# A two-layer decoder on one core: last norms in two parts, routing in pieces between the shared products, slots written out

## The chip, the cores and the metric

The kernel runs on one core of a Trainium2 chip. The metric is the device time of one execution in microseconds; the median of three runs is given beside the time of the one execution that was profiled. Engines are named as in the profile: PE is TensorE, PEld its weight loads, DVE is VectorE, ACT is ScalarE, POOL is GpSimd, SP is SyncE.

## What is computed

Four sequences of 512 tokens with 512 features, 2048 tokens in all, pass six residual parts, each followed by a layer norm without weights. The change touches the last two parts and the norms behind them:

```
x = _layernorm(x + _L1_xattn_ref(ctx_512, x, Wq, Wk, gamma))      # graph stage
x = _layernorm(x + _L1_ffn_ref(x, router_w, router_bias, Wu, Wg, Wd, Su, Sg, Sd))

# graph:  sim >= threshold of the 153 largest of its row; A = sigmoid(sim) * mask
#         A = (A + A transposed) / 2;  result (1 - g) * x + g * A
# experts:
logits = flat @ router_w.T                       # 16 experts
scores = softmax(logits); topk_idx = top_k(logits + router_bias, 2)
combine = the two scores of the chosen experts, divided by their sum
for e in range(16):
    out += combine[:, e:e + 1] * ((silu(flat @ Wu[e]) * (flat @ Wg[e])) @ Wd[e])     # 256 wide
out += (silu(flat @ Su) * (flat @ Sg)) @ Sd                                          # shared, 512 wide
```

## The kernel before

X stays in SBUF as 16 tiles of 128 tokens (four batches of four). Each stage is a block in which every engine has its own straight list of instructions and waits on semaphores; nothing orders the work but these lists and waits. There is a barrier between stages. Before the part that matters here come two self attentions, a cross attention, a quantised feed-forward stage, and a search for the graph's thresholds.

Products that need more than one pass of precision take a matrix as a high part (a copy in the type fp32r) and a low part (the rest); H stands for high, L for low in the names. The high part is written by ScalarE, the low one is a subtraction on VectorE (or POOL), and a product is three matmuls: high by high, low by high, high by low.

**Graph stage** (stage_graph, L1470). A loop over four batches: ScalarE computes SIGM and XS, VectorE masks them (L1584), PE transposes (L1522), VectorE adds (L1591), mixes into X (L1597) and takes statistics (L1600). Behind the loop VectorE computes mean and 1/deviation of all 16 tiles in 25 small steps (L64 to L77, each waits for the one before) and applies them to 16 tiles (L1605).

**route_and_share** (L1637). PE turns X (L1867) into two PSUM places UG; ScalarE and VectorE write XTH and XTL (L1743, L1768). Logits: for each of 16 token tiles twelve matmuls, XT standing in the array and the router's 16 columns moving (L1876). Then VectorE routes: two best experts per token (L1780, L1781), their shares, per-tile counts from PE (L1884, L1885), running sums BEFORE (L1801), first tile of each expert (L1806), slots (L1808 to L1818), the expert of each slot tile (L1823 to L1826). After its last step (semaphore routed at ROUTE) two things start: POOL scatters the token numbers into a table in HBM with 32 indirect DMAs (L1731), which SP then reads back, and VectorE and PE begin the shared expert. That has two halves j of 256 hidden columns; per half the weights are converted in one piece (L1751, L1841), and then for each of four batches m PE does up_gate (48 matmuls, L1895) and down of the batch before (24, L1908); ScalarE does the silu (L1755) and the high part of H (L1758), VectorE the product H (L1848), its low part (L1852) and the addition to X (L1835, gather).

**run_slots** (L1924). Tokens sorted by expert fill 48 tiles of 128 slots, each with one expert. Per tile POOL fetches 128 token rows (XG, L1986) and the expert's weights (RAW, 128 x 3072, L1988) into rings of four places; ScalarE writes WH in three copies (two of the up part L2060, down L2072), VectorE the low part of the first up half (L2089) and of down (L2121), POOL that of the second up half (L1993). PE does twelve up products (L2144), turns the next tokens (L2132) and the hidden rows (L2159), and does six down products (L2178); VectorE copies the result to YS (L2118), SP stores it. The indirect DMAs read their row numbers from PICK, which VectorE fills (L2080, L2081) since the tile's number is a loop variable. The first four and the last five steps are written out, the others run in a loop of four steps. POOL issues the fetch for tile t+3 in step t when down_lo shows tile t-1 done.

**combine_slots** (L2185). POOL gathers two rows per token (32 indirect DMAs, L2207, ring of four), VectorE adds them with their shares (L2216), takes statistics (L2219) and, after the last, norms as in the graph stage (L2224). Behind a barrier store_x writes X in one DMA of 4.2 MB (L2268).

## Time and profile before

| | us |
|---|---|
| median of 3 runs (2809.75 to 2814.63) | 2813.01 |
| the profiled execution | 2814.64 |
| its span, first to last instruction | 2812.7 |
| busy in the span: PE, DVE, ACT, POOL | 2066.3, 1822.6, 1217.9, 801.8 |
| logits, 2167.8 to 2209 | 41.2 |
| routing and first weights, 2209 to 2244.6 | 35.6 |
| shared expert, 2244.6 to 2388.4 | 143.8 |
| slots, 2388.4 to 2735.7 | 347.3 |
| combination, norm and store, 2735.7 to 2812.7 | 77.0 |

Times in the trace count from the start of the span. A window's row gives the busy time of each engine in a stretch, the mean clock that TensorE was granted as a share of 2.4 GHz (0.50 is 1.2 GHz), the share of the time in which packets were under way on the 16 DMA engines (packets may overlap, so it can pass 1) and what they moved. A row of the timeline gives start, duration, engine, line, operation, tiles, the count of merged instructions, and in brackets the idle time of the engine before it with what ended it.

### The profile page before, as it was taken

The page shows a single profiled execution, that of the slowest core. Times are in us where ns is not written, and L with a number is a line of the kernel's source. Part 1 is how long each engine was busy: PE and PEld are TensorE (multiplying, and loading weights), DVE is VectorE, ACT ScalarE, POOL GpSimd, SP SyncE. Part 2 cuts the span into 40 slices and gives each one's busy share as a digit, 9 for nine tenths or more (in the row PEclk, how much of TensorE's full clock was granted, in tenths as well). Part 3 has the DMA queues.
Part 4 walks back from the last instruction along what each step waited for, and adds up shares of the span by engine and source line. Part 5 has one row for each costly group of instructions (what it writes and reads, how often), then busy time and mean ns, then how long its engine had stood idle before and what let it go on. Part 6 is the DMA issues. An engine that isn't in the chain of part 4 may idle for free. (4 is left out here: it accounts for less than half of the span.)

```text
span 2812.7 us, 34294 instructions
## 1 busy us (share of the span) xinstructions
PE 2066.3 (73%) x12308; PEld 1398.0 (50%) x12308; DVE 1822.6 (65%) x2851; ACT 1217.9 (43%) x2168; POOL 801.8 (29%) x712
## 2 busy tenths in 40 slices
PE   5999997386877886899847999994014589677760
PEld 4778775122222223555526777772003477555540
DVE  3456555476767757899963555654885433788876
ACT  2332222285556563677762322321862021556540
POOL 1211322106577511121111212131000130666654
PEclk8999998589889888999967999997555599999995
DMA  4422221655244204000013223221002000899965
GB/s 142 98 56 59 57 58 23 180 173 144 90 127 121 61 12 170 1 1 1 1 38 98 64 50 69 52 62 60 0 0 107 1 1 0 308 307 303 305 223 164
DMA packets 84875, 266.48 MB, mean 95 GB/s; under 512 B 17488, under 2 KB 19024, under 8 KB 73600
## 3 DMA queue, kind: packets, MB, share of 16 engines
q0 software_dynamic: 29856, 153.33, 18.2%
q1 hardware_dynamic: 53856, 111.01, 13.9%
q8 instruction: 89, 1.46, 0.2%
q10 hardware_dynamic: 1024, 0.26, 0.0%
q14 instruction: 50, 0.41, 0.0%
HBM read 171.70 MB, written 41.99 MB: 76 GB/s over the span
## 5 line engine op out<-in xcount | busy, mean ns | idle before, releaser
L875 DVE TENSOR_REDUCE x_negm<-x_M 128x2 f32<-128x1024 f32 x256 | 309.3, 1223 | 115.4 <-PE x_M L935 114.9
L824 ACT ACTIVATE x_PT<-x_T 128x512 f32<-128x512 f32 x512 | 280.2, 598 | 210.8 <-PE x_T L955 206.0
L317 ACT ACTIVATE L_attn_PT<-L_attn_T 128x512 f32<-128x512 f32 x320 | 175.4, 595 | 357.9 <-PE L_attn_T L519 357.7
L387 DVE TENSOR_REDUCE L_attn_negm<-L_attn_M 128x2 f32<-128x1024 f32 (+1 forms) x192 | 191.8, 1041 | 56.5 <-PE L_attn_M L500 56.2
L224 POOL DMA_DIRECT2D L_attn_QKS<-L_attn_HL x64 | 34.9, 546 | 598.0 <-ACT L_attn_HL L302 564.3
L955 PE MATMUL x_T<-x_QS,x_KS 49*128 49x512 f32 x512 | 144.0, 559 | 64.0 <-ACT x_PT L824 43.7
L517 PE MATMUL L_attn_T<-L_attn_QKS 97*128 97x256 f32 (+3 forms) x512 | 164.6, 383 | 10.2 <-DMA L_attn_QKS<-L_attn_mT 7.9
L964 PE MATMUL x_O<-x_PT,x_V 128*32 128x512 f32 x1024 | 160.7, 704 | 7.6 <-issue 7.6
L955 PEld LDWEIGHTS x_T<-x_QS,x_KS 49*128 49x128 f32 x512 | 53.0, 204 | 217.5 <-ACT x_PT L824 135.9
L935 PE MATMUL x_M<-x_KS,x_QS 48*128 48x512 f32 x512 | 120.7, 468 | 42.8 <-DMA x_QS<-x_xl 23.3
L498 PE MATMUL L_attn_M<-L_attn_QKS 96*128 96x384 f32 (+2 forms) x384 | 134.8, 420 | 19.2 <-DVE L_attn_XTL L361 11.5
L1522 PE MATMUL graph_P<-ident,graph_L 128*128 128x128 f32 x64 | 15.7, 428 | 173.0 <-DVE graph_L L1584 167.8
L2060 ACT ACTIVATE slots_WH<-slots_RAW 128x1024 fp32r<-128x1024 f32 x94 | 94.6, 1054 | 100.3 <-DMA slots_RAW<-in_experts,slots_PICK 100.3
L2121 DVE TENSOR_TENSOR slots_WL<-slots_RAW,slots_WH 128x1024 fp32r<-128x1024 f32 x48 | 130.9, 2726 | 0.2 <-ACT slots_WH L2072 0.2
L434 PE MATMUL L_attn_M<-L_attn_XTH,L_attn_WH 128*128 128x512 f32 x256 | 109.1, 426 | 16.3 <-DVE L_attn_XTL L361 16.3
L519 PE MATMUL L_attn_T<-mask_kq,identr 128*128 128x128 f32 x512 | 120.4, 247 | 0.0
L1993 POOL TENSOR_TENSOR slots_WL<-slots_RAW,slots_WH 128x1024 fp32r<-128x1024 f32 x48 | 116.3, 2423 | 10.5 <-ACT slots_WH L2060 5.6
L1534 ACT ACTIVATE graph_seen_a<-graph_SIM,graph_mid 128x512 bf16<-128x512 f32 x128 | 90.5, 708 | 59.1 <-DMA graph_SIM<-graph_sim 39.8
L517 PEld LDWEIGHTS L_attn_T<-L_attn_QKS 97*128 97x128 f32 x512 | 104.8, 205 | 17.0 <-DMA L_attn_QKS<-L_attn_mT 9.1
L405 DVE RECIPROCAL L_attn_AQ<-L_attn_DEN 128x512 f32<-128x512 f32 x32 | 107.2, 3349 | 7.1 <-PE L_attn_O L537 7.1
L434 PE MATMUL L_attn_M<-L_attn_XTH,L_attn_WL 128*128 128x512 f32 x256 | 106.4, 416 | 0.0
L1986 POOL DMA_INDIRECT slots_XG<-moe_x_rows,slots_PICK x48 | 48.6, 1012 | 201.7 <-DVE slots_PICK L2081 200.9
(377 smaller groups left out, 5711.9 us busy)
## 6 DMA issues: line engine op xcount, KB each, us to landing
L_attn_QKS<-L_attn_HL SPq DMA_DIRECT2D x192, 128.0 KB, 4.7
L_attn_QKS<-L_attn_HL POOLq DMA_DIRECT2D x192, 128.0 KB, 4.1
moe_y_rows<-slots_YS SPq DMA_DIRECT2D x48, 256.0 KB, 7.6
x_WRAW<-in_w_gateT POOLq DMA_DIRECT2D x8, 1024.0 KB, 7.5
x_QS<-x_xh SPq DMA_DIRECT2D x128, 64.0 KB, 2.4
x_WRAW<-in_w_upT POOLq DMA_DIRECT2D x8, 1024.0 KB, 5.6
x_WRAW<-in_w_downT POOLq DMA_DIRECT2D x8, 1024.0 KB, 5.9
ffn_w<-x_WTER POOLq DMA_DIRECT2D x12, 512.0 KB, 3.6
```

Source lines behind the costliest of these rows:

```text
L317: ac.activation(PT[:, s, bank], T[:, bank], ACT.Exp, scale=SCALE).then_inc(t_free, 1)
L387: last = ve.tensor_reduce(negm[:, g % 2, h0:h0 + nh, i], src, AX.X, ALU.max, negate=True)
L434: inst = pe.matmul(out, lhs(a, k), rhs(a, k), start=(n == 0), stop=(n == len(passes) - 1))
L498: pe.matmul(m[:, c:c + w], QKS[0:R, r, 0, h, P * i:P * (i + 1)], QKS[0:R, r, 1, h, 0:w], start=True, stop=False)
L517: pe.matmul(T[:, c:c + w], QKS[0:R + 1, r, 1, h, P * j:P * (j + 1)], QKS[0:R + 1, r, 0, h, P * j:S], start=True, stop=False)
L519: last = pe.matmul(T[:, c:c + P], C["identr"][:], C["mask_kq"][:], start=False, stop=True)
L824: ac.activation(PT[:, s // 4, head(s), :], T[(STEPS_S * g + s) % 3][:], ACT.Exp, scale=SCALE).then_inc(t_free, 1)
L875: ve.tensor_reduce(negm[:, g % 2, u // 4:4:2, u % 4], m[:].rearrange("p (r k) -> p r k", r=2), AX.X, ALU.max, negate=True).then_inc(m_free, 1)
L935: last = pe.matmul(m[:, BANK * r:BANK * (r + 1)], QS[rows, g % 4, u // 4, P * (u % 4):P * (u % 4 + 1)], KS[rows, g % KV, :], start=True, s ...
L955: pe.matmul(T[(STEPS_S * g + s) % 3][:], KS[rows, g % KV, P * j:P * (j + 1)], QS[rows, g % 4, head(s) % 2, :], start=True, stop=True).then ...
L964: last = pe.matmul(O[VW * h:VW * (h + 1), :], V[:, (g // KV) % 2, j, g % KV, :], PT[:, j, h, :], start=(j == 0), stop=(j == NT - 1))
L2121: ve.tensor_tensor(WL[i % 2][:, DOWN], RAW[i][:, DOWN], WH[i % 2][:, DOWN].bitcast(F32), ALU.subtract).then_inc(q["down_lo"], 1)
```

## The change

- **Last norms.** In the graph stage and in the combination, the small steps are done in two parts: for tiles 0 to 11 (EARLY = 12) before the last batch's work, for 12 to 15 behind it. A 26th step makes shift = -mean * rstd (emit_shift). ScalarE applies the first 14 tiles (norm_tile), VectorE the last two. The store is part of the combination's block: SP stores each batch when its tiles are done, the last one in two halves. The graph's loop over batches is written out.
- **Turning and logits.** X is turned into four PSUM places (TURN) instead of two. The router's weights stand in the array (16 columns), 512 token columns move: 48 matmuls instead of 192. The result is 16 x 2048; ScalarE copies it out (LT) and PE turns it back by 16 transposes.
- **Routing in pieces.** The shared weights are converted in two pieces (2048 up columns, 1024 down columns), the first pieces directly behind the logits. PE starts the shared products then and does the counting products behind up_gate(0, 1); VectorE's routing is cut into functions that stand between its operations of the shared expert. The counts are copied out of PSUM (take_counts), and PE waits for that before down(0, 0). The second half's weights are converted during the last products of the first.
- **Slots.** All steps are written out; 47 tiles instead of 48; rings of six places; POOL only issues the fetches, with row numbers straight from slot_token and weight_row (no PICK); VectorE does the low part of both up halves; ScalarE copies the result to YS, one step later.

```diff
+            def norm_tile(t):
+                ac.activation(XF[:, t, :], XF[:, t, :], ACT.Identity, scale=rstd[:, t:t + 1],
+                              bias=shift[:, t:t + 1]).then_inc(q["applied"], 1)
...
+            act.wait_ge(q["shifted"], 1)
+            for t in range(EARLY):
+                norm_tile(t)
+            act.wait_ge(q["shifted"], 2)
+            for t in range(EARLY, EARLY + NT // 2):
+                norm_tile(t)
+            act.wait_ge(q["applied"], EARLY + NT // 2)
...
+                if b == NB - 1:
+                    moments(0, 0, EARLY)
...
-    SLOT_TILES = 2 * NTILE + NE
+    SLOT_TILES = 2 * NTILE + NE - 1
...
+        TURN = UG + Y
...
+            for v in range(2):
+                act.wait_ge(q["lt_full"], 2 * v + 2)
+                ac.activation(LT[:, 2 * BANK * v:2 * BANK * (v + 1)], UG[v][0:NE, :], ACT.Copy).then_inc(q["lt_taken"], 1)
+            for part in range(2):
+                weights_hi(0, part)
...
+                assert route.n == TAKEN
+
+            def first_tiles():
+                route(ve.memset(BEFORE[:, 0, :], 0.0))
+                for t in range(NTILE):
+                    route(ve.tensor_tensor(BEFORE[:, t + 1, :], BEFORE[:, t, :], COUNT[:, t, :], ALU.add))
...
+            weights_lo(0, 0)
...
+            best_two(0, 8)
+            hidden(0, 0, 0)
+            best_two(8, NTILE)
+            hidden(0, 0, 1)
+            choices()
+            hidden_lo(0, 0, 0)
+            hidden_lo(0, 0, 1)
+            weights_lo(0, 1)
+            hidden(0, 1, 0)
+            shares()
+            hidden(0, 1, 1)
+            take_counts()
+            hidden_lo(0, 1, 0)
+            hidden_lo(0, 1, 1)
...
+            first_tiles()
+            for i in range(NT):
+                gather(0, 0, i)
+            hidden(0, 2, 0)
+            slot_places()
+            hidden(0, 2, 1)
+            hidden_lo(0, 2, 0)
+            hidden_lo(0, 2, 1)
+            for i in range(NT):
+                gather(0, 1, i)
+            tile_experts()
...
+                if m == NB - 1:
+                    if j == 0:
+                        weights_lo(1, 0)
+                    for i in range(NT):
+                        gather(j, m, i)
+                    if j == 0:
+                        weights_lo(1, 1)
...
+                if n >= 4:
+                    t_.wait_ge(q["xt_lo"], n - 3)
...
-            for t in range(NTILE):
+            for b in range(NB):
+                t_.wait_ge(q["xt_lo"], max(2 * b + 2, 5 + b // 2))
+                if b >= 2:
+                    t_.wait_ge(q["xt_lo"], 2 * NB)
                 n = 0
-                for xp, wp in ((XTH, RWL), (XTL, RWH), (XTH, RWH)):
+                for wp, xp in ((RWL, XTH), (RWH, XTL), (RWH, XTH)):
                     for k in range(KC):
-                        last = pe.matmul(Y[0][:, NE * t:NE * (t + 1)], xp[:, k, P * t:P * (t + 1)], wp[:, k, :],
-                                         start=(n == 0), stop=(n == 3 * KC - 1))
+                        last = pe.matmul(UG[b // 2][0:NE, BANK * (b % 2):BANK * (b % 2 + 1)], wp[:, k, :],
+                                         xp[:, k, S * b:S * (b + 1)], start=(n == 0), stop=(n == 3 * KC - 1))
                         n += 1
+                last.then_inc(q["lt_full"], 1)
+            for v in range(2):
+                t_.wait_ge(q["lt_taken"], v + 1)
+                for t in range(2 * NT * v, 2 * NT * (v + 1)):
+                    last = pe.transpose(Y[0][:, NE * t:NE * (t + 1)], LT[:, P * t:P * (t + 1)], C["ident"][0:NE, 0:NE])
             last.then_inc(q["logits"], 1)
...
-            t_.wait_ge(q["routed"], ROUTE)
-            with t_.Fori(0, 2) as j:
-                t_.wait_ge(q["w_lo"], j + 1)
+            for j in range(2):
                 for m in range(NB):
                     up_gate(j, m)
+                    if j == 0 and m == 1:
+                        t_.wait_ge(q["made"], 8)
+                        t_.wait_ge(q["routed"], SORTED)
+                        mask = MASK[:].rearrange("p t e -> p (t e)")
+                        pe.matmul(Y[1][:, 0:NTILE * NE], earlier[:], mask, start=True, stop=True)
+                        pe.matmul(Y[1][:, BANK:BANK + NTILE * NE], ones[:], mask, start=True,
+                                  stop=True).then_inc(q["counted"], 1)
+                        t_.wait_ge(q["routed"], TAKEN)
                     if m > 0:
                         down(j, m - 1)
                 down(j, NB - 1)
...
-    RING = 4
-    TURNS = SLOT_TILES // RING
+    RING, LAST = 6, SLOT_TILES - 1
...
-                        if not isinstance(t, int):
-                            pool.sem_inc(q["between"], 1)
-                        pool.wait_ge(q["down_lo"], t)
-                        if not isinstance(t, int):
-                            pool.sem_inc(q["between"], 1)
-                        pool.wait_ge(q["up_lo_pool"], t)
-                    if not isinstance(t, int):
-                        pool.sem_inc(q["between"], 1)
-                    fetch(t + RING - 1, i + RING - 1)
...
+            for t in range(SLOT_TILES):
+                n = t % RING
+                if t >= RING:
+                    pool.wait_ge(down_lo, t - RING + 1)
+                    pool.wait_ge(up_lo, 2 * (t - RING + 1))
+                pool.indirect_dma_start(out=XG[n], out_offset=None, in_=T["x_rows"],
+                                        in_offset=bass.IndirectOffsetOnAxis(T["slot_token"][:, t:t + 1], 0)
+                                        ).then_inc(x_in[n], 16)
+                pool.indirect_dma_start(out=RAW[n], out_offset=None, in_=weights,
+                                        in_offset=bass.IndirectOffsetOnAxis(T["weight_row"][:, t:t + 1], 0)
+                                        ).then_inc(w_in[n], 16)
...
+            def take_y(t):
+                act.wait_ge(y_full, t + 1)
+                if t >= 4:
+                    act.wait_ge(y_out[t % 4], 16 * (t // 4))
+                ac.activation(YS[t % 4], Y[t % 2][:], ACT.Copy).then_inc(y_taken, 1)
+
+            up_weights(0)
+            turned(0)
+            for t in range(SLOT_TILES + 2):
+                if t < LAST:
+                    up_weights(t + 1)
+                if 1 <= t <= SLOT_TILES:
+                    act.wait_ge(ht_full, t)
+                    ac.activation(HH[:], HT[:, 0:F], ACT.Copy).then_inc(h_hi, 1)
+                if t >= 2:
+                    take_y(t - 2)
+                if t < LAST:
+                    turned(t + 1)
+                if t <= LAST:
+                    act.wait_ge(u_full, t + 1)
+                    ac.activation(SU[t % 2], U[t % 2][:, 0:F], ACT.Silu).then_inc(silu_done, 1)
+                    if t >= 2:
...
+            for t in range(SLOT_TILES + 1):
+                if t < LAST:
+                    up_rest(t + 1, 0)
+                if t >= 1:
+                    dve.wait_ge(h_hi, t)
+                    ve.tensor_tensor(HL[:], HT[:, 0:F], HH[:].bitcast(F32), ALU.subtract).then_inc(h_lo, 1)
+                if t < LAST:
+                    up_rest(t + 1, 1)
+                    turned_rest(t + 1)
+                if t <= LAST:
+                    dve.wait_ge(silu_done, t + 1)
+                    ve.tensor_tensor(H[t % 2], SU[t % 2], U[t % 2][:, F:], ALU.mult).then_inc(h_made, 1)
+                    dve.wait_ge(down_hi, t + 1)
+                    ve.tensor_tensor(WL[t % 2][:, DOWN], RAW[t % RING][:, DOWN], WH[t % 2][:, DOWN].bitcast(F32),
+                                     ALU.subtract).then_inc(down_lo, 1)
...
             for t in range(NTILE):
+                if t == EARLY:
+                    moments(0, 0, EARLY)
...
+            moments(1, EARLY, NTILE)
+            for t in range(EARLY + NT // 2, NTILE):
+                ve.tensor_scalar(XF[:, t, :], XF[:, t, :], mean[:, t:t + 1], rstd[:, t:t + 1],
+                                 ALU.subtract, ALU.mult).then_inc(applied_v, 1)
...
+        @block.sync
+        def _(sp):
+            for b in range(NB - 1):
+                sp.wait_ge(applied_a, NT * (b + 1))
+                sp.dma_start(out[:, b, :, :], X[:, b, :, :]).then_inc(x_out, 16)
+            sp.wait_ge(applied_a, EARLY + NT // 2)
+            sp.dma_start(out[:, NB - 1, 0:NT // 2, :], X[:, NB - 1, 0:NT // 2, :]).then_inc(x_out, 16)
+            sp.wait_ge(applied_v, NT // 2)
+            sp.dma_start(out[:, NB - 1, NT // 2:, :], X[:, NB - 1, NT // 2:, :]).then_inc(x_out, 16)
+            sp.wait_ge(x_out, 16 * (NB + 1))
```

**TensorE, from the turning of X to the first shared product.** Before (share_UG and share_Y are PSUM places, the last two numbers the shape written):

```order
L1867 MATMUL share_UG<-ident,X 128x128 x64
L1876 MATMUL share_Y<-share_RWL,share_XTH 128x16 x4
L1876 MATMUL share_Y<-share_RWH,share_XTL 128x16 x4
L1876 MATMUL share_Y<-share_RWH,share_XTH 128x16 x4
...
L1884 MATMUL share_Y<-share_routing,share_earlier 128x256
L1885 MATMUL share_Y<-share_routing,share_ones 128x256
```

After:

```order
L1967 MATMUL share_Y<-ident,X 128x128 x16
L1978 MATMUL share_UG<-share_XTH,share_RWL 16x512 x4
L1978 MATMUL share_UG<-share_XTL,share_RWH 16x512 x4
L1978 MATMUL share_UG<-share_XTH,share_RWH 16x512 x4
...
L1985 MATMUL share_Y<-ident,share_LT 128x16 x16
L1999 MATMUL share_UG<-share_XTH,share_WH 128x512 x4
```

The group of three rows of logits stands 16 times before and 4 times now, and the counting products no longer stand between the logits and the first shared product.

**VectorE, from the sorted choices on.** Before:

```order
L1791 TENSOR_TENSOR share_routing<-share_routing 128x256
L1793 TENSOR_TENSOR share_total<-moe_share 128x16
L1794 RECIPROCAL share_total<-share_total 128x16
L1796 TENSOR_TENSOR moe_share<-moe_share,share_total 128x16 x2
L1799 MEMSET share_BEFORE 128x16
L1801 TENSOR_TENSOR share_BEFORE<-share_BEFORE,share_Y 128x16 x16
L1802 TENSOR_SCALAR share_tiles_i<-share_BEFORE 128x16
L1803 TENSOR_SCALAR share_tiles_i<-share_tiles_i 128x16
L1804 CAST share_tiles_f<-share_tiles_i 128x16
```

After:

```order
L1853 TENSOR_TENSOR share_routing<-share_routing 128x256
L1831 TENSOR_TENSOR share_HL<-share_H,share_HH 128x512 x2
L1819 TENSOR_TENSOR share_WL<-share_RAW,share_WH 128x1024
L1827 TENSOR_TENSOR share_H<-share_SU,share_UG 128x512
L1857 TENSOR_TENSOR share_total<-moe_share 128x16
L1858 RECIPROCAL share_total<-share_total 128x16
L1860 TENSOR_TENSOR moe_share<-moe_share,share_total 128x16 x2
L1827 TENSOR_TENSOR share_H<-share_SU,share_UG 128x512
L1865 COPY share_WITHIN<-share_Y 128x256
L1866 COPY share_COUNT<-share_Y 128x256
L1831 TENSOR_TENSOR share_HL<-share_H,share_HH 128x512 x2
L1870 MEMSET share_BEFORE 128x16
```

The routing's steps keep their order; between them now stand the low parts and products of the shared expert's first two batches, and the two copies out of PSUM.

**VectorE, one step of the slots.** Before (the loop's register instructions left out):

```order
L2080 COPY slots_PICK<-moe_slot_token 128x1
...
L2081 COPY slots_PICK<-moe_weight_row 128x1
...
L2089 TENSOR_TENSOR slots_WL<-slots_RAW,slots_WH 128x1024
L2104 TENSOR_TENSOR slots_HL<-slots_HT,slots_HH 128x256
L2085 TENSOR_TENSOR slots_XTL<-slots_XT,slots_XTH 128x512
L2109 TENSOR_TENSOR slots_H<-slots_SU,slots_U 128x256
L2118 COPY slots_YS<-slots_Y 128x512
L2121 TENSOR_TENSOR slots_WL<-slots_RAW,slots_WH 128x1024
```

After (the two rows of L2148 are the two up halves):

```order
L2148 TENSOR_TENSOR slots_WL<-slots_RAW,slots_WH 128x1024
L2159 TENSOR_TENSOR slots_HL<-slots_HT,slots_HH 128x256
L2148 TENSOR_TENSOR slots_WL<-slots_RAW,slots_WH 128x1024
L2143 TENSOR_TENSOR slots_XTL<-slots_XT,slots_XTH 128x512
L2165 TENSOR_TENSOR slots_H<-slots_SU,slots_U 128x256
L2167 TENSOR_TENSOR slots_WL<-slots_RAW,slots_WH 128x1024
```

The picks and the copy of YS have gone, and a third subtraction of 128x1024 stands between HL and XTL.

## Rows read from the trace of the kernel before

**Rows 1.** Windows by stage: length, busy us (instructions) per engine, clock, DMA share, GB/s.

```profile
core 0: us, PE busy (x) PEld busy (x) DVE busy (x) ACT busy (x) POOL busy (x), PEclk, DMA share, GB/s
2079.00:2149.40 70.40, 15.73 (x64) 12.55 (x64) 55.80 (x97) 18.78 (x32) 0.00 (x0) 0.50 0.00 0
2150.40:2167.80 17.40, 11.33 (x64) 9.52 (x64) 9.78 (x9) 9.51 (x10) 1.31 (x8) 0.79 0.92 328
2167.80:2209.00 41.20, 41.10 (x192) 41.04 (x192) 0.00 (x0) 0.00 (x0) 0.00 (x0) 0.50 0.12 45
2209.00:2244.60 35.60, 2.05 (x5) 1.19 (x5) 29.54 (x129) 5.74 (x4) 3.23 (x1) 0.50 0.00 0
2244.60:2312.30 67.70, 67.69 (x288) 55.52 (x288) 20.50 (x31) 9.39 (x16) 30.96 (x32) 0.97 0.02 2
2312.30:2320.20 7.90, 0.02 (x1) 0.03 (x1) 4.05 (x2) 5.33 (x3) 0.00 (x0) 0.83 0.00 0
...
2400.00:2411.00 11.00, 6.91 (x24) 5.44 (x25) 5.70 (x11) 7.00 (x10) 6.80 (x4) 0.72 1.01 414
...
2440.00:2700.00 260.00, 202.60 (x912) 151.89 (x912) 227.68 (x303) 154.37 (x227) 164.05 (x114) 1.00 0.91 304
...
2735.70:2784.40 48.70, 0.00 (x0) 0.00 (x0) 35.16 (x48) 0.00 (x0) 34.19 (x32) 0.50 0.61 172
...
2801.00:2811.00 10.00, 0.00 (x0) 0.00 (x0) 0.00 (x0) 0.00 (x0) 0.00 (x0) 0.50 1.03 386
```

**Rows 2.** Timeline, end of graph stage: start, us, engine, line, operation, tiles, count, [idle].

```profile
2120.47 2.56 ACT L1550 ACTIVATE graph_XS<-X,graph_g 128x512 f32 x4 [7.86 <-DVE X L1597]
...
2126.02 1.23 DVE L1591 TENSOR_TENSOR graph_SUM<-graph_P,graph_L 128x1024 f32<-128x1024 f32 x1 [2.13 <-PE graph_P L1522]
...
2134.83 0.18 DVE L64 TENSOR_TENSOR graph_mean<-graph_stats 128x16 f32<-128x16 f32 x1
...
2140.08 9.28 DVE L1605 TENSOR_SCALAR X<-X,graph_mean,graph_rstd 128x512 f32<-128x512 f32 x16
```

**Rows 3.** Timeline, VectorE, turning X.

```profile
2154.33 2.35 DVE L1768 TENSOR_TENSOR share_XTL<-share_UG,share_XTH 128x1024 fp32r<-128x1024 f32 x2 [0.69 <-ACT share_XTH L1743]
```

**Rows 4.** Timeline, TensorE, first shared products, low clock, then high.

```profile
2244.59 2.07 PE L1895 MATMUL share_UG<-share_XTH,share_WH 128*128 128x512 f32 x4 [20.21 <-DVE share_WL L1841]
...
2249.56 1.07 PE L1895 MATMUL share_UG<-share_XTH,share_WH 128*128 128x512 f32 x4
```

**Rows 5.** Tile share_WH: duration ns min/median/max, first and last start.

```profile
L1751 ACT ACTIVATE share_WH<-share_RAW x2: 2762/2762/2762, 2212.6 to 2313.8; 128x3072 fp32r x2
...
L1841 DVE TENSOR_TENSOR share_WL<-share_RAW,share_WH x2: 3359/3360/3360, 2241.1 to 2316.7; 128x3072 fp32r<-128x3072 f32 x2
```

**Rows 6.** Tile moe_table: POOL's scatters, same columns.

```profile
L1731 POOL DMA_INDIRECT moe_table<-share_token_id,share_place x32: 957/962/4092, 2241.4 to 2284.0; - x32
```

**Rows 7.** Groups by shape, 2410 to 2720: busy us, mean ns, idle before.

```profile
L2121 DVE TENSOR_TENSOR slots_WL<-slots_RAW,slots_WH 128x1024 fp32r<-128x1024 f32 x46 | 128.4, 2792 | 0.2 <-ACT slots_WH L2072 0.2
...
L2089 DVE TENSOR_TENSOR slots_WL<-slots_RAW,slots_WH 128x1024 fp32r<-128x1024 f32 x46 | 55.7, 1211 | 1.1 <-ACT slots_WH L2060 1.1
...
L2118 DVE COPY slots_YS<-slots_Y 128x512 f32<-128x512 f32 x45 | 31.1, 692 | 37.2 <-PE slots_Y L2178 37.2
...
L2036 ACT ACTIVATE slots_XTH<-slots_XT 128x512 fp32r<-128x512 f32 x45 | 26.8, 595 | 27.1 <-PE slots_XT L2132 26.7
```

**Rows 8.** Waits, 2410 to 2720: us in total, times, longest.

```profile
ACT slots_WH L2060 <- DMA slots_RAW<-in_experts,slots_PICK: 97.2, 44, 3.4
```

**Rows 9.** DMA queues, 2440 to 2700: packets, MB, share of 16 engines.

```profile
q0 software_dynamic: 8464, 69.15, 81.1%
q1 hardware_dynamic: 5468, 9.96, 9.9%
```

**Rows 10.** Timeline, combination: POOL's gather beside VectorE.

```profile
2740.70 1.43 POOL L2207 DMA_INDIRECT combine_YG<-moe_y_rows,moe_slot  x1 [0.30 <-issue]
...
2740.57 1.54 DVE L2216 SCALAR_TENSOR_TENSOR X<-combine_YG,moe_share,X 128x512 f32<-128x512 f32 x2 [8.71 <-DMA combine_YG<-moe_y_rows,moe_slot]
```

564 lines of the change are left out of this document (259 added, 305 removed).

## Prediction

> **What bounds the kernel now.** I read the windows by stage first, since the change touches only the last 734 us of a 2812.7 us span (from the graph stage's normalisation at 2134.8 on), and different things end each stretch there [rows 1]. The reader should see five stretches. (a) The end of the graph stage is VectorE alone. (b) 2167.8 to 2209: TensorE is busy for all of its 41.2 us, but with 192 products of only 16 columns, at a granted 0.50 (1.2 GHz). (c) 2209 to 2244.6: TensorE has 5 matmuls in 35.6 us; VectorE works on the routing and then on the weights' low part. (d) 2244.6 to 2388: shared products back to back, 67.7 us for each of the two weight halves, with a hole of 7.9 us between them. (e) 2440 to 2700, the slots' steady part: 38 tiles in 260 us, 6.84 each; nothing is full (TensorE 5.33 us a tile, VectorE 5.99, ScalarE 4.06, POOL 4.32), and DMA shows a share of 0.91 at 304 GB/s. A tile moves 128 x 3072 x 4 bytes of weights and twice 128 x 512 x 4, 2.10 MB. Then come the combination (POOL 34 of 49 us), the norm and a store that nothing overlaps.
>
> The slots need a closer look. ScalarE waits 97.2 us in 44 times for weights to land [rows 8]: 2.2 us a tile. That does not say yet that bandwidth is the limit. A fetch for tile t+3 goes out only when VectorE has finished tile t-1's down part. One form explains much of VectorE's load: the down subtraction takes 2792 ns, while the same shape on another line takes 1211 [rows 7]. It runs while POOL does its own 128x1024 subtraction; and every time it is late, the next fetch is late. So fetch, conversion, subtraction and fetch form a ring of four places: 27.4 us round, 6.84 a tile.
>
> **The change, part by part**, against the profiled execution (span 2812.7, 2814.6 in all; the median of the runs is 2813.0, 1.6 less).
>
> 1. Graph norm. Before: 25 small steps from 2134.83 to 2140.08 (0.21 each), then 16 tiles in 9.28 us [rows 2]. After: 26 steps for 12 tiles go ahead of the last batch's sums, 5.5 us, of which 2.13 lie in the wait for TensorE that stands there anyway; +3.3. Behind the last statistics 26 steps more, 5.5, then two tiles on each of two engines; ScalarE's take 0.64 each (2.56 for 4 [rows 2]), 1.3. Its first 12 tiles (7.7 us) lie beside VectorE's last 8.8 + 5.5. Sum: 3.3 + 5.5 + 1.3 = 10.1 against 14.5: **-4.4**. Unrolling the four batches itself gains nothing: VectorE shows no gap at a turn.
>
> 2. Turning X. Two PSUM places become four. VectorE then is the bound: eight subtractions at 1.18 (2.35 for two [rows 3]), the first 3.9 us in, done at 13.3 instead of 17.4. TensorE is ahead, done turning after about 10.4. Logits: 48 products of 512 columns instead of 192 of 16. Four such products take 2.07 us from start to end at the low clock and 1.07 at the high one, and follow each other each 0.91 at the latter [rows 4], 0.226 a product: 10.9 us. In the turning of before TensorE was busy 11.3 of 17.4 us, in pieces with waits between, and had a mean of 0.79; now it turns almost without a hole, so I take the high clock. Logits' end comes 10.4 + 10.9 = 21.3 after the start instead of 58.6: **-37.3**. At the low clock the 48 take 21.8, 10.9 more.
>
> 3. From logits to the first shared product. Before 35.6 us [rows 1]: all the routing, then the subtraction of 3.36 [rows 5]. After: the copy of 16x1024 out of PSUM, not in the trace (bounds 0.6, a 128x512 PSUM copy, to 1.1; 1.1 taken, since a 128x1024 PSUM read takes 1.0); conversion of 2048 of 3072 columns, 1.84; its subtraction, 2.24 [rows 5]; 0.15 to start. 5.3 in all: **-30.3**. The 16 small turns hide beside the conversion.
>
> 4. Routing between the shared products. VectorE's routing costs 29.5 - 3.4 = 26 us [rows 1], and it is busy only 20.5 of 67.7 us in a half. Let T be the first product. Walking VectorE's new list with the old durations: the choices (MASK) are ready at T+18; TensorE reaches the counting products at T+24; they take 1.0 to 2.0, and TensorE then waits until VectorE, which first takes hidden(0,1,1), has copied both counts out: T+26.8. **+2.8**. Slots' places are known at T+43, the last step at T+55. POOL then scatters 32 times at 0.96 + 0.3 [rows 6] plus the table's way back, until about T+102, where the shared products run until T+136. Cover left: 33 us; if it is gone, the excess counts in full.
>
> 5. Between the halves. TensorE's 7.9 us hole [rows 1] goes: the first 2048 columns are converted and subtracted during down(0,3), which frees nothing else late. With it goes the restart at the low clock, (2.07 - 1.07) over the first ten or so products, 2.5. **-10.4**.
>
> 6. Slots. One tile fewer, six places instead of four, POOL fetches only, VectorE gets POOL's half and gives the output copy to ScalarE. VectorE a tile: 5.99 - (2.79 - 1.21) - 0.69 (copy [rows 7]) - 0.2 (two picks) + 1.21 = 4.7. ScalarE 4.06 + 0.60 (its PSUM copies of 128x512 [rows 7]) = 4.7. TensorE stays at 5.33. In the loop of TensorE's order, turning the next tokens, ScalarE's copy, VectorE's rest and the next product give 5.2 to 5.3 a tile. DMA: bounds are 5.07 (2.10 MB at the 414 GB/s of 2400 to 2411, when fetches stood in line [rows 1]) and 6.22 (the packets' own time: 81.1% + 9.9% of 6.84 [rows 9]), with 6.84 if nothing improves. With six places fetches stand in line as in the fast stretch, but writes are mixed in as in the slow one: I take 5.6, nearer the former, since in the slow one each fetch waited for VectorE before it was issued, and six places end that. 46 steps of 5.6 against 47 of 6.81: 257.6 against 320.0, **-62.4**. Start and tail stay.
>
> 7. Combination and store. VectorE reaches tile 12 with 12 tiles summed; 26 steps, 5.5, go in ahead of it. POOL's gathers run on meanwhile, so VectorE has the last four tiles in hand and takes 2.3 each; last statistics 4.2 us later than before. Then 5.5 + 1.3, and the last 0.5 MB: 1.4 at 386 GB/s [rows 1] plus 1.5 fixed (the 4.2 MB store landed in 12.4, of which 10.9 are data at that rate). From the old end of statistics 4.2 + 6.8 + 2.9 + 0.8 = 14.7 instead of 28.3: **-13.6**.
>
> Sum: -4.4 - 37.3 - 30.3 + 2.8 - 10.4 - 62.4 - 13.6 = -155.6. 2814.6 - 155.6 - 1.6 = **2657**.
>
> A rule that speaks against part 6. POOL's gather that began at 2740.70 took 1.43 instead of 0.95 and ended at 2742.13, just when VectorE's two operations with two SBUF inputs ended at 2742.11 [rows 10]; others there with the same overlap did too. The Trainium skill (SBUF — State Buffer, SBUF: two separate sides) says that VectorE and GpSimd share a port pair as an exclusive lock, and that GpSimd cannot write the descriptors of its DMAs meanwhile. By that rule, the trace agrees; here it would stretch each fetch and not the sum, since POOL has 5.6 us for two.
>
> **The rivals.**
> A. DMA stays the limit. For it: 0.91 share, ScalarE's waits [rows 8]. Against: 414 GB/s were reached. At 6.22 a tile: 46 x 0.62 = 29 more, 2686; at 6.84 only the one tile is saved: 57 more, 2714.
> B. Engines and DMA are both better than taken: 5.1 to 5.3, 2634 to 2643.
> C. The logits run at the low clock: +11, 2668; it adds to any case.
> D. Slower. In the slots, VectorE now runs three 1.21 us subtractions with two SBUF inputs, 3.6 us a tile. If each of POOL's two fetches were held until all of that has passed, and more fetches did not help: 2 x (1.26 + 3.63) = 9.8 a tile, 46 x 4.2 = 193 more, 2850. It outweighs the other gains from 5.6 + 156/46 = 9.0 a tile on. Against: a held gather lost 0.5, not 3.6, and VectorE's list has three operations a tile with at most one SBUF input.
> E. The pieces don't fit: VectorE is late for the silu products and TensorE stands 10 to 30 us in the first half, or the scatter sticks out. 2667 to 2690. My walk shows one place only.
> F. The change does not do what it says: long straight code is fetched in the slots while the DMA queues are full, and engines stand for it. In 2440 to 2700 of before only one instruction packet was needed; straight code elsewhere ran without such holes, but under less traffic. 1 us a tile would be 46: 2703. The Trainium skill (Runtime: NRT & Kernel Launch, Instruction fetch mechanics) says that straight code is fetched ahead and taken branches are what stalls; no row here shows either under full queues.
>
> **How the numbers follow.** Forecast with 5.3 to 5.9 a tile 0.55 (2643 to 2671); A 0.25; B 0.06; E 0.06; F 0.05; D 0.03; C is inside the others (0.3). A measurement of this kernel tells 0.2% (5.6 us) from no change. All but D and the extremes of F and E end far below that: faster 0.95, same 0.01, slower 0.04. The range reaches from B's floor to A's ceiling: 2634 to 2714.
>
> **What would show each step.** Logits of about 11 us at clock 1.0; the first shared product near 2173; no hole between halves, one of 3 us at the counting products; the last scatter ahead of the last shared product; steady tiles 5.6 apart, VectorE's down subtraction back at 1.21, DMA near 370 GB/s; the last store 0.5 MB. The prediction is wrong if the steady tiles stay above 6.3 apart, if VectorE in the shared stage makes TensorE wait in more than one place, or if POOL's fetches take more than 2 us each.

## The result, and the profile after

The changed kernel takes 2624.3 us, the median of 4 runs (2621.3 to 2635.8), against 2813.8 before (2809.8 to 2814.7): a ratio of 0.936, 95% interval 0.933 to 0.938. The prediction was 2657 with a range of 2634 to 2714: the direction was right, and the time is 9.7 us below the low end. The profiled execution took 2622.4 us with a span of 2620.7, 192.0 less than before's. One later execution of the changed kernel took 3171.7 us at a mean granted clock of 0.617, against 0.867 to 0.872 in all its others, and is left out of every comparison.

The windows by stage of the changed kernel (length, busy us and instructions of each engine, TensorE's clock, DMA share, GB/s), from the first masked product of the graph stage on; the rows of before are in [rows 1]:

```profile
core 0: us, PE busy (x) PEld busy (x) DVE busy (x) ACT busy (x) POOL busy (x), PEclk, DMA share, GB/s
2066.28:2128.20 61.92, 15.74 (x64) 12.55 (x64) 52.16 (x110) 28.08 (x45) 0.00 (x0) 0.50 0.00 0
2128.20:2155.56 27.36, 22.08 (x128) 14.55 (x128) 11.71 (x11) 13.88 (x14) 1.34 (x8) 0.87 0.78 276
2155.56:2293.40 137.84, 134.40 (x580) 110.52 (x580) 73.02 (x197) 23.35 (x36) 33.40 (x32) 0.98 0.01 1
2293.40:2556.70 263.30, 240.96 (x1128) 183.64 (x1128) 230.70 (x282) 215.88 (x329) 131.39 (x94) 0.97 0.92 375
2556.70:2620.70 64.00, 0.00 (x0) 0.00 (x0) 44.80 (x102) 10.09 (x14) 33.71 (x32) 0.50 0.64 197
```

In the third row (the shared expert) the shared products now fill 134.4 of 137.8 us; in the fourth (the slots) TensorE is busy for 241 of 263 us, where before it idled over a fifth of the slots' steady part. Cut at the same marks in both traces, the 192 us go like this:

| stretch (marks) | before, us | after, us | difference | predicted |
|---|---|---|---|---|
| start to the graph's first masked product | 2080.1 | 2066.3 | -13.8 | 0 |
| to the end of the graph's norm | 69.3 | 61.9 | -7.4 | -4.4 |
| to the first shared product | 95.2 | 27.4 | -67.8 | -67.6 |
| to the first slot fetch | 145.4 | 138.1 | -7.3 | -7.6 |
| to the first gather of the combination | 345.7 | 263.1 | -82.6 | -62.4 |
| to the end of the span | 77.0 | 63.9 | -13.1 | -13.6 |

Three rows are off: the first, in code that the change doesn't touch; the second by 3 us; the slots by 20.

How the third row of the table came out is seen in TensorE's timeline (start, us, line, operation, tiles, shapes, count, [idle before]):

```profile
2129.35 3.65 PE L1967 MATMUL share_UG<-ident,X 128*128 128x128 f32 x16 [12.84 <-PEq L48]
...
2139.05 1.09 PE L1978 MATMUL share_UG<-share_XTH,share_RWL 128*16 128x512 f32 x4
...
2149.25 1.09 PE L1978 MATMUL share_UG<-share_XTH,share_RWH 128*16 128x512 f32 x4
...
2151.44 0.67 PE L1985 MATMUL share_Y<-ident,share_LT 16*128 16x16 f32 x8 [0.51 <-ACT share_LT L1796]
2155.56 1.65 PE L1999 MATMUL share_UG<-share_XTH,share_WH 128*128 128x512 f32 x3 [3.46 <-DVE share_WL L1819]
```

Turning takes 9.6 us, the 48 logit products 11.3 at the high clock (four in 0.93), and 5.2 us later the first shared product starts.

The slots' steady part, 2350 to 2500, by groups (busy us, mean ns of one, idle before), to be held against [rows 7]:

```profile
L2148 DVE TENSOR_TENSOR slots_WL<-slots_RAW,slots_WH 128x1024 fp32r<-128x1024 f32 x59 | 71.8, 1217 | 0.0
L2108 ACT ACTIVATE slots_WH<-slots_RAW 128x1024 fp32r<-128x1024 f32 x60 | 60.2, 1059 | 0.0
L2086 POOL DMA_INDIRECT slots_XG<-moe_x_rows,moe_slot_token x29 | 48.9, 1685 | 55.7 <-DVE slots_WL L2167 55.7
...
L2167 DVE TENSOR_TENSOR slots_WL<-slots_RAW,slots_WH 128x1024 fp32r<-128x1024 f32 x30 | 36.8, 1226 | 6.0 <-ACT slots_WH L2137 6.0
```

The down subtraction is back from 2792 ns to 1226. ScalarE's first copy (L2108) has no idle time before it: the wait of 2.2 us a tile for the weights [rows 8] is gone. Now POOL waits, 1.9 us a tile, because the ring is full. The windows' row for the same 150 us names the new bound:

```profile
2350.00:2500.00 150.00, 148.01 (x703) 113.26 (x703) 143.52 (x176) 134.30 (x205) 84.13 (x58) 1.00 1.02 417
```

TensorE is busy for 148.0 of 150 us, VectorE for 143.5. So busy time alone does not say which of the two sets the tile; fewer_products below does. A tile's order on TensorE, one tile of the timeline:

```profile
2452.11 1.17 PE L2186 MATMUL slots_U<-slots_WH,slots_XTH 128*128 128x512 f32 x4
2453.11 1.08 PE L2186 MATMUL slots_U<-slots_WH,slots_XTL 128*128 128x512 f32 x4
2454.03 0.38 PE L2200 MATMUL slots_HT<-ident,slots_H 128*128 128x128 f32 x2
2454.17 1.18 PE L2186 MATMUL slots_U<-slots_WL,slots_XTH 128*128 128x512 f32 x4
2455.18 0.60 PE L2177 MATMUL slots_XT<-ident,slots_XG 128*128 128x128 f32 x4
2455.54 0.71 PE L2218 MATMUL slots_Y<-slots_WH,slots_HH 128*128 128x512 f32 x2
```

There is no idle time in it of 0.1 us or more. The 18 products of 512 columns follow each other at 0.23 us within a group and the six turns at 0.11, which makes 4.8 us (an estimate from these spacings); the rest of the tile goes at the changes from one group to the next. From the first to the last H product on VectorE (2313.4 to 2548.1, 46 steps) a tile takes 5.10 us.

The end, from the timeline: the moments of the first twelve tiles, the last norm and the last store.

```profile
2594.38 0.18 DVE L64 TENSOR_TENSOR combine_mean<-combine_stats 128x12 f32<-128x12 f32 x1
...
2599.97 8.57 ACT L2280 ACTIVATE X<-X,combine_shift,combine_rstd 128x512 f32<-128x512 f32 x12 [47.05 <-DVEq L2261]
...
2608.84 0.17 DVE L64 TENSOR_TENSOR combine_mean<-combine_stats 128x4 f32<-128x4 f32 x1
...
2616.04 0.47 SPq L2298 DMA_DIRECT2D out_x<-X  x1
```

### The profile page after: what moved, and what is told of

Read it like the earlier page. It is cut to its first block and busy times, and to the rows that moved or that the text cites. A ratio compares the mean times of both kernels' runs of the same rounds, so it can differ in the third digit from the quotient of the medians.

```text
span 2620.7 us, 32973 instructions
## 1 busy us (share of the span) xinstructions
PE 2007.4 (77%) x12156; PEld 1348.8 (51%) x12156; DVE 1763.1 (67%) x2779; ACT 1255.1 (48%) x2238; POOL 719.4 (27%) x662
## 3 DMA queue, kind: packets, MB, share of 16 engines
q10 hardware_dynamic: 1024, 0.26, 0.0%
## 5 line engine op out<-in xcount | busy, mean ns | idle before, releaser
L392 DVE TENSOR_REDUCE L_attn_negm<-L_attn_M 128x2 f32<-128x1024 f32 (+1 forms) x192 | 192.0, 1041 | 57.3 <-PE L_attn_M L505 56.9
L2148 DVE TENSOR_TENSOR slots_WL<-slots_RAW,slots_WH 128x1024 fp32r<-128x1024 f32 x94 | 114.3, 1217 | 13.8 <-ACT slots_WH L2108 13.8
L439 PE MATMUL L_attn_M<-L_attn_XTH,L_attn_WH 128*128 128x512 f32 x256 | 109.4, 427 | 15.8 <-DVE L_attn_XTL L366 15.8
L2086 POOL DMA_INDIRECT slots_XG<-moe_x_rows,moe_slot_token x47 | 75.8, 1613 | 124.2 <-DVE slots_WL L2167 82.9
L524 PEld LDWEIGHTS L_attn_T<-mask_kq,identr 128*128 128x128 f32 x512 | 106.1, 207 | 0.2
L439 PE MATMUL L_attn_M<-L_attn_XTL,L_attn_WH 128*128 128x512 f32 x256 | 105.2, 411 | 0.0
```

Of the source, the lines that this page charges most:

```text
L392: last = ve.tensor_reduce(negm[:, g % 2, h0:h0 + nh, i], src, AX.X, ALU.max, negate=True)
L439: inst = pe.matmul(out, lhs(a, k), rhs(a, k), start=(n == 0), stop=(n == len(passes) - 1))
L524: last = pe.matmul(T[:, c:c + P], C["identr"][:], C["mask_kq"][:], start=False, stop=True)
L2148: ve.tensor_tensor(WL[t % 2][:, cols], RAW[t % RING][:, cols], WH[t % 2][:, cols].bitcast(F32), ALU.subtract).then_inc(up_lo, 1)
```

## The experiments

Three questions are open. Is the first row of the table the change's doing? What made the slot tile 5.10 us and not 5.6: the ring of six, POOL's freed engine, or the written-out tiles? And are the other terms worth what they were predicted to be worth, or did errors cancel? Since the time of the untouched part differs from run to run by some us (below), the runs are compared by stretches of their traces first: "from the graph on" is the time from the first masked product of the graph stage to the end of the span (554.4 us in the changed kernel, 554.1 when it was profiled again, 732.6 before), and the us a tile are the 46 or 47 steps between the first and the last H product of the slots. Five kernels ran once only: fewer_products (2611.6 us), fewer_products_and_subtractions (2619.3), ring5 (2634.2), before_moved_work_only (2767.6) and before_graph_unrolled (2814.2). Their whole times carry no interval, and what is said of them rests on the stretches.

| kernel | us a tile | from the graph on | against the changed kernel |
|---|---|---|---|
| before | 6.74 | 732.6 | +178.2 |
| changed | 5.10 | 554.4 | |
| ring4 | 5.96 | 593.8 | +39.4 |
| ring5 | 5.11 | 554.6 | +0.2 |
| pool_subtracts | 6.28 | 608.0 | +53.6 |
| fewer_products | 4.91 | 543.8 | -10.6 |
| fewer_products_and_subtractions | 4.91 | 543.1 | -11.3 |
| before_moved_work_only (48 tiles) | 6.09 | 700.1 | -32.5 against before |
| before_graph_unrolled | 6.76 | 731.0 | -1.6 against before |
| router_moving | 5.10 | 580.9 | +26.5 |
| routing_first | 5.10 | 571.3 | +16.9 |
| fetch_two_early | 5.10 | 544.6 | -9.8 |

### The changed kernel again: whose are the first 13.8 us?

> The changed kernel once more, unaltered, for the spread of its time and for the cross-attention stage, which the change does not touch. Eight profiles so far have that stage end between 1037.3 and 1059.1 us, three of kernels built on the one before (1037.3, 1050.9, 1052.8) and seven of kernels built on the changed one (1037.3 three times, 1045.2, 1046.8, 1048.1, 1059.1 and so on). Theory V, the clock granted to TensorE falls at other places from run to run: the five times spread over 10 us or more, and the mean clock of a run is lower where its time is longer. Rival P, the place of the code in the program sets it: the stage ends at 1037 to 1039 us again and the times agree within 3 us.

Five runs lie between 2623.1 and 2631.4 us, median 2626.4, ratio 0.937 (0.935 to 0.939). In eleven runs beside them before lay between 2800.2 and 2820.5, median 2805.6. So a kernel's time spreads over 8 to 20 us from run to run. Its mean clock goes with it only roughly: 2623.1 us at 0.871 and 2630.9 at 0.867, but the slowest, 2631.4, at 0.869; 2800.2 at 0.859 and 2820.5 at 0.851 for before. The cross-attention stage, the same code in all kernels, ended in the traces at these times (last score product of the stage):

| built on | us |
|---|---|
| before | 1050.9 (before itself), 1037.3, 1052.8 |
| changed | 1037.6 (the changed kernel itself), 1041.7 (again), 1037.3, 1037.3, 1044.3, 1045.2, 1046.8, 1048.1, 1048.2, 1059.1 |

A kernel built on before reached 1037.3, and ones built on the changed kernel 1048 and 1059. Where the time goes is seen in the clock of two windows of that stage, of before and then of the changed kernel:

```profile
700.00:850.00 150.00, 118.86 (x645) 40.41 (x645) 110.57 (x185) 84.25 (x157) 93.63 (x30) 0.83 0.36 102
...
937.10:1050.90 113.80, 92.76 (x503) 29.52 (x499) 73.73 (x127) 68.91 (x130) 22.96 (x9) 0.84 0.11 26
```

```profile
700.00:850.00 150.00, 116.36 (x684) 39.90 (x678) 115.69 (x198) 89.12 (x167) 93.99 (x31) 0.91 0.36 103
...
924.80:1037.60 112.80, 89.96 (x532) 29.36 (x529) 78.36 (x130) 73.21 (x138) 28.36 (x9) 0.92 0.13 35
```

In the same 150 us the changed kernel did 684 products and before 645, at 0.91 of the clock instead of 0.83. From that last score product to the graph's first masked product all 13 traces take 1028.4 to 1029.6 us, so the stage makes nearly the whole spread of the path ahead. Its mean clock was 0.83 in the two that ended last and 0.87 to 0.89 in the four that ended first, with 0.86 to 0.87 and no clear order between them. Rival P fails: the stage ended at 1041.7 and not at 1037 to 1039, and the times do not agree within 3 us. Theory V is the better reading, though the five times spread over 8.3 us and not the 10 it asked for. What makes the clock fall at other places is not shown. A kernel built on before also reached 1037.3, so these us are not the change's. All four runs of before beside the result were long for it (2809.8 to 2814.7); its later medians were 2804.4 to 2805.6. The later medians differ by 179.2 us (2805.6 and 2626.4), and the stretches from the graph on by 178.2: this, and not 192, is what the change is worth.

### Ring of 4

```diff
-    RING, LAST = 6, SLOT_TILES - 1
+    RING, LAST = 4, SLOT_TILES - 1
```

> The changed kernel with a ring of 4 slot tiles in place of 6, nothing else. In the changed kernel a slot tile takes 5.11 us, TensorE is busy 99% of the stretch, and GpSimd waits 1.9 us in each tile for a ring place that VectorE frees. Theory T, TensorE's own work sets the tile: 5.1 to 5.2 us a tile, within 5 us of the changed kernel's 2624 us. Rival R, the deeper ring made the gain over the predicted 5.6 us: 5.4 to 5.7 us a tile, 14 to 28 us longer, with ScalarE's copies waiting for the weights' transfer.

2669.0 us (ratio 0.950, 0.946 to 0.955). 5.96 us a tile and 39.4 us longer from the graph on, outside both theories and on rival R's side (5.4 to 5.7, 14 to 28 us): with four places the weights come late, by more than R said. Waits, 2400 to 2530 (us in total, times, longest):

```profile
POOL slots_XG L2086 <- DVE slots_WL L2167: 68.9, 22, 5.5
ACT slots_WH L2108 <- DMA slots_RAW<-in_experts,moe_weight_row: 22.3, 16, 3.0
```

POOL waits 3.1 us for a place, and then ScalarE 1.0 us a tile for the transfer. Theory T in the form "TensorE alone sets the tile" is wrong for four places.

### Ring of 5

```diff
-    RING, LAST = 6, SLOT_TILES - 1
+    RING, LAST = 5, SLOT_TILES - 1
```

> The changed kernel with a ring of 5. The ring of 4 gave 5.96 us a tile with ScalarE waiting 1.0 us in each for the weights' transfer (9.6 us from issue to landing), the ring of 6 gave 5.10, where TensorE is busy 99%. If a ring of n lets a fetch start n - 2.4 tiles ahead of its use, and that must cover the 9.6 us: 4 places give 9.6/1.6 = 6.0 us a tile, as measured, and 5 places allow 3.7, so that TensorE sets 5.1 us. If the time falls evenly with the places: 5.5 us.

5.11 us a tile, and TensorE busy for 128.2 of 130 us: with five places the transfer is covered, and the sixth buys nothing. The time does not fall evenly with the places; it falls until the next bound. That the same formula gave 6.0 for four was fitted, so only the five are a test of it.

### POOL subtracts again

```diff
+            def rest(t):
+                pool.wait_ge(up_hi, 2 * t + 2)
+                gp.tensor_tensor(WL[t % 2][:, PARTS[1]], RAW[t % RING][:, PARTS[1]],
+                                 WH[t % 2][:, PARTS[1]].bitcast(F32), ALU.subtract).then_inc(up_lo_pool, 1)
...
+            for t in range(SLOT_TILES):
+                if t + RING - 1 <= LAST:
+                    fetch(t + RING - 1)
+                if t < LAST:
+                    rest(t + 1)
```

> The changed kernel with the second half of each slot tile's up-weight subtraction given back to GpSimd, behind its fetches, as before the change; the ring of 6, ScalarE's copy of Y and the written-out tiles stay. Theory S, GpSimd and VectorE stretch each other when both read two SBUF operands: VectorE's down-weight subtraction takes 2.4 to 2.8 us in place of 1.23, VectorE's sum is then 1.22+2.8+0.69+0.43+0.41 = 5.55 us and GpSimd's 2.4+2.0 and its waits; 5.6 to 6.0 us a tile, 24 to 40 us longer. Rival T, TensorE is the bound and has room for both: 5.1 to 5.2 us a tile, no longer than the changed kernel.

2682.4 us (ratio 0.956, 0.953 to 0.960); 6.28 us a tile, more than even theory S gave. Groups, 2400 to 2530:

```profile
L2097 POOL TENSOR_TENSOR slots_WL<-slots_RAW,slots_WH 128x1024 fp32r<-128x1024 f32 x21 | 53.9, 2568 | 0.4
L2166 DVE TENSOR_TENSOR slots_WL<-slots_RAW,slots_WH 128x1024 fp32r<-128x1024 f32 x21 | 49.6, 2361 | 0.0
L2185 DVE TENSOR_TENSOR slots_WL<-slots_RAW,slots_WH 128x1024 fp32r<-128x1024 f32 x21 | 44.7, 2129 | 3.0 <-ACT slots_WH L2153 2.0
```

The means of VectorE's two subtractions are 2361 and 2129 ns, from 1217 and 1226. They are means of two kinds, as POOL's and VectorE's timelines show:

```profile
2463.26 2.72 POOL L2097 TENSOR_TENSOR slots_WL<-slots_RAW,slots_WH 128x1024 fp32r<-128x1024 f32 x1
2469.16 2.42 POOL L2097 TENSOR_TENSOR slots_WL<-slots_RAW,slots_WH 128x1024 fp32r<-128x1024 f32 x1
```

```profile
2462.51 1.23 DVE L2185 TENSOR_TENSOR slots_WL<-slots_RAW,slots_WH 128x1024 fp32r<-128x1024 f32 x1
2463.65 3.41 DVE L2166 TENSOR_TENSOR slots_WL<-slots_RAW,slots_WH 128x1024 fp32r<-128x1024 f32 x1
...
2469.55 3.11 DVE L2185 TENSOR_TENSOR slots_WL<-slots_RAW,slots_WH 128x1024 fp32r<-128x1024 f32 x1 [0.20 <-ACT slots_WH L2153]
2472.59 1.21 DVE L2166 TENSOR_TENSOR slots_WL<-slots_RAW,slots_WH 128x1024 fp32r<-128x1024 f32 x1
```

In each tile one of VectorE's two keeps its 1.22 us, and the other, which falls on POOL's, takes 3.1 to 3.4. The latter ends 1.08 to 1.09 us behind POOL's end (2465.98 and 2467.06, 2471.58 and 2472.66), and so do 31 of the 33 long ones between 2390 and 2610. It is as if it stood until POOL is done and then ran. In the kernel before, the long down subtractions [rows 7] do the same: 28 of 29 end 1.08 to 1.09 us behind POOL's. VectorE does one subtraction less and is still busy 117.7 of 130 us. Work that seems to be taken off an engine is paid for twice: the two engines' sum of 128x1024 subtractions is 7.06 us a tile in place of 3.66. ScalarE no longer waits for transfers there, yet the tile is only 0.46 us shorter than before's: while VectorE stands so long, a deep ring is of little use.

### The moved work alone, in the kernel before

```diff
-            rest(0, 0)
...
-                if has(t, 0, SLOT_TILES - 2):
-                    rest(t + 1, i + 1)
...
+            def up_rest_2(t, i):
+                dve.wait_ge(q["up_hi"], 2 * t + 2)
+                ve.tensor_tensor(WL[i % 2][:, PARTS[1]], RAW[i % RING][:, PARTS[1]],
+                                 WH[i % 2][:, PARTS[1]].bitcast(F32), ALU.subtract).then_inc(q["up_lo_pool"], 1)
...
-                    ve.tensor_copy(YS[n], Y[(i - 1) % 2][:]).then_inc(q["y_taken"], 1)
+                ac.activation(YS[n], Y[i % 2][:], ACT.Copy).then_inc(q["y_taken"], 1)
```

> The kernel before with two edits in its slot stage alone: VectorE subtracts the second half of the up weights in place of GpSimd, and ScalarE copies Y in place of VectorE. The looped tiles, the ring of 4, the copied indices and the 48 tiles stay. It stands against the changed kernel's slots with a ring of 4 (5.88 us a tile, waiting for the weights' transfer). Theory R, the ring of 4 sets that rate whether the tiles are looped or written out: 5.8 to 6.1 us a tile against 6.81, 35 to 48 us less than before. Rival L, the loop's register operands and its extra waits cost as well: 6.2 to 6.6 us a tile, 10 to 30 us less.

6.09 us a tile, inside theory R's range, and its slot stage is shorter than before's by 31.7 us, a little under the 35 to 48 that R said. Against ring4, written out and with the picks gone, it is 0.13 us a tile slower. So of before's 6.74: moving the two pieces of work (POOL's subtraction to VectorE and VectorE's copy to ScalarE; they were not run apart) brings 0.65 at a ring of four, writing the tiles out without picks 0.13, and the larger ring 0.86, all but 0.01 of it with the fifth place. The order matters: with POOL still subtracting, six places, written-out tiles and the moved copy together bring 0.46. Neither the moved work alone (0.65) nor the rest without POOL's subtraction (0.46) gets half of the 1.64.

### Fewer products, then fewer subtractions

```diff
-                    ups = [(xp, wp, k) for xp, wp in ((XTH[i], WH[i]), (XTL[i], WH[i]), (XTH[i], WL[i]))
+                    ups = [(xp, wp, k) for xp, wp in ((XTH[i], WH[i]), (XTL[i], WH[i]))
...
-                    for hp, wp in ((HH, WH[r]), (HL, WH[r]), (HH, WL[r])):
+                    for hp, wp in ((HH, WH[r]), (HL, WH[r])):
```

> The changed kernel, leaving out of every slot tile the six products with the weights' low part (four up, two down); the subtractions that make the low part stay. A slot tile then has 12 products and 6 turns on TensorE. Theory T, TensorE is the bound and VectorE the next (4.88 us busy in a tile): 4.9 us a tile and about 10 us less. Rival A of the prediction, the transfers stand at their limit (5.07 us a tile at 414 GB/s): 5.05 to 5.11 us a tile, less than 3 us gained.

> As the run before, and the three subtractions of the weights' low part cut to 64 of their 1024 columns. VectorE is then busy about 2 us in a tile, ScalarE 4.6 and TensorE under 4, so that either ScalarE or the transfers set the tile. If the transfers' limit is the predicted 5.07 us: 5.05 to 5.11 us a tile. If it is lower: 4.6 to 4.7 us a tile, set by ScalarE, some 22 us less than the changed kernel, and the rate read from the trace is then a lower bound for what the transfers can do.

4.91 us a tile in both, although VectorE is busy 126.2 of 130 us in the one and 52.9 in the other. The first run alone had looked like VectorE as the next bound, with the very number that theory T gave for it; the second shows that it isn't. What both have in common (waits of the two kernels, 2400 to 2530):

```profile
ACT slots_WH L2108 <- DMA slots_RAW<-in_experts,moe_weight_row: 13.2, 26, 0.9
```

```profile
ACT slots_WH L2108 <- DMA slots_RAW<-in_experts,moe_weight_row: 13.1, 27, 0.5
```

A second sign is the time of a weights' fetch from issue to landing between 2400 and 2530: 10.0 us in the changed kernel, 16.3 and 18.5 in these two, so the fetches stand in line. The transfers set 4.91 us, 2.10 MB at 427 GB/s (the packets of the second run's trace give 423). Theory T got the number right and its reason wrong, and the second run fell between what its two theories said. The prediction's lowest bound, 5.07 at 414 GB/s, was read from a stretch of 11 us and was not the limit. The changed kernel stands 0.19 us a tile above the transfers' limit, where TensorE's 24 operations hold it.

### The graph's batches written out, in the kernel before

```diff
-            with dve.Fori(0, NB) as b:
+            for b in range(NB):
...
-                    ve.scalar_tensor_tensor(out=L[:, i, :], in0=SIM[:, b * NT + i, :], scalar=low[:, bass.ds(b * NT + i, 1)],
+                    ve.scalar_tensor_tensor(out=L[:, i, :], in0=SIM[:, b * NT + i, :], scalar=low[:, b * NT + i:b * NT + i + 1],
```

> The kernel before with the four batches of the graph stage written out in place of a loop on ScalarE and VectorE, nothing else. The prediction said that this gains nothing: the first mask products stay 13.7 us apart. The changed kernel has them 12.9 us apart, so the other theory, that an operand indexed by the loop's register makes each such instruction start later, says 12.9 us, 2.4 us over the three intervals and about 3 us in all.

The batches are 12.9 us apart instead of 13.7, and from the first masked product to the norm's end it is 66.3 us instead of 69.3 (1.3 of these us are lost again behind it, 1.0 of them in its slots at 6.76 us a tile, which the edit does not touch). VectorE's timeline, first of before, then of this kernel:

```profile
2086.30 0.75 DVE L1597 SCALAR_TENSOR_TENSOR X<-graph_SUM,graph_gh,graph_XS 128x512 f32 x1
2087.20 0.69 DVE L1600 BATCH_NORM_STATS2 graph_stats<-X  x1
```

```profile
2087.42 0.75 DVE L1598 SCALAR_TENSOR_TENSOR X<-graph_SUM,graph_gh,graph_XS 128x512 f32<-128x512 f32 x1
2088.20 0.69 DVE L1601 BATCH_NORM_STATS2 graph_stats<-X 128x6 f32<-128x512 f32 x1
```

The operations take the same 0.75 and 0.69 us, but in the loop the second starts 0.90 us after the first, and 0.78 without. Of the 0.78 us that a batch takes longer in the loop, about 0.6 lie at its six steps that wait for the one before (0.09 to 0.12 each), and 0.13 at the loop's turn; neither shows as idle time of a group. The four masks, whose operand is indexed by the register as well but which do not wait for each other, start 0.66 us apart in both kernels. The edit takes the register out of the operands and out of the counts that the waits compare with, and which of the two costs is not shown. The remaining 4.4 us of the graph term are the norm in two parts.

### Moving router weights

```diff
-                for wp, xp in ((RWL, XTH), (RWH, XTL), (RWH, XTH)):
+                for xp, wp in ((XTH, RWL), (XTL, RWH), (XTH, RWH)):
                     for k in range(KC):
-                        last = pe.matmul(UG[b // 2][0:NE, BANK * (b % 2):BANK * (b % 2 + 1)], wp[:, k, :],
-                                         xp[:, k, S * b:S * (b + 1)], start=(n == 0), stop=(n == 3 * KC - 1))
+                        last = pe.matmul(Y[0][:, NE * t:NE * (t + 1)], xp[:, k, P * t:P * (t + 1)], wp[:, k, :],
+                                         start=(n == 0), stop=(n == 3 * KC - 1))
```

> The changed kernel with the logits made as before the change: per tile of tokens, the turned tokens stand as weights and the 16 router columns move, 192 products, with no turning back of the logits and after all turned tiles are in. Theory, the products' number sets it: about 0.21 to 0.25 us each, 41 to 48 us in place of the 11.5 us that the four wide groups and the turning back take, so 28 to 38 us longer than the changed kernel. Rival, most of the predicted gain was the clock (this stretch stood at 1.2 GHz before the change, and here it comes right behind 128 turns at 2.4 GHz): at 2.4 GHz the 192 products take 20 to 25 us, and the kernel is 8 to 15 us longer.

2656.4 us (ratio 0.946, 0.942 to 0.950), 26.5 us longer from the graph on: a little under the theory's 28 to 38, and well over the rival's 8 to 15. Its windows, turning and then the narrow products, and TensorE's timeline where the one ends and the other begins:

```profile
2154.00:2164.00 10.00, 6.41 (x51) 5.69 (x50) 9.18 (x9) 7.41 (x8) 0.00 (x0) 0.96 0.95 352
2164.00:2174.00 10.00, 9.99 (x52) 10.00 (x52) 2.29 (x1) 4.14 (x3) 0.00 (x0) 0.55 0.93 359
2174.00:2204.00 30.00, 30.00 (x142) 30.00 (x143) 0.00 (x0) 0.00 (x0) 0.00 (x0) 0.50 0.01 1
```

```profile
2158.26 2.22 PE L1964 MATMUL share_Y<-ident,X 128*128 128x128 f32 x16
2164.01 0.58 PE L1973 MATMUL share_Y<-share_RWL,share_XTH 128*128 128x16 f32 x4 [3.52 <-DVE share_XTL L1904]
```

Behind the turns TensorE stands for 3.5 us, since this order waits for all turned tiles. The clock falls at 2165.0, 1.0 us after the first narrow product, and is 0.50 to the last one at 2204.2, with TensorE busy throughout by its records. It is back at 2209.4, behind 5.2 us of shared products with 512 moving columns. The changed kernel has a wait of 3.5 us too, ahead of its first shared product, and its clock is also low behind it, but it is back 5.1 us after that product starts (2155.6 to 2160.7). So the fall may be the wait's doing in both; that narrow products brought it about is not shown. What is shown is that 39 us of products with 16 moving columns did not bring the clock back, and some 5 us of wide ones did. So the low clock of before's logits [rows 1] needs no waits inside them. The form costs twice: in the number of instructions, and in the clock. The first products, still at the high clock, start 0.11 us apart and the later ones 0.21, so 192 of them take 40.2 us and would take about 21 at the high clock (an estimate from the 0.11).

### All routing first

```diff
             best_two(0, 8)
-            hidden(0, 0, 0)
             best_two(8, NTILE)
-            hidden(0, 0, 1)
             choices()
+            shares()
+            take_counts()
+            dve.wait_ge(q["copied"], 16)
+            first_tiles()
+            slot_places()
+            tile_experts()
+            hidden(0, 0, 0)
+            hidden(0, 0, 1)
```

with the two counting products ahead of the first shared product.

> The changed kernel with VectorE's whole routing, and TensorE's two counting products, ahead of the first shared product in place of in pieces between them. The prediction puts the end of routing 31 us behind the logits and the gain of the pieces at 30.3 us plus 10.4 us for the hole between the halves that is cut separately, less 2.8 us for the wait for the counts. Theory: 25 to 31 us longer, since only the wait ahead of the first product comes back (26 to 30 us) and the counting wait of 2.8 us goes. Rival: the pieces on VectorE delay the shared products as much as they hide, 0 to 10 us longer.

2644.4 us (ratio 0.943, 0.938 to 0.947), 16.9 us longer from the graph on, between what the two theories gave. TensorE's timeline tells why:

```profile
2169.27 1.06 PE L2024 MATMUL share_Y<-share_routing,share_ones 128*128 128x256 f32 x2
2171.37 2.08 PE L1999 MATMUL share_UG<-share_XTH,share_WH 128*128 128x512 f32 x4 [1.04 <-DVE share_COUNT L1866]
...
2184.31 1.07 PE L1999 MATMUL share_UG<-share_XTH,share_WL 128*128 128x512 f32 x4
2188.25 2.05 PE L1999 MATMUL share_UG<-share_XTH,share_WH 128*128 128x512 f32 x4 [2.88 <-DVE share_H L1827]
```

In this kernel TensorE needs only the counts to be read, not the whole routing, so the first 48 shared products (2171.4 to 2185.3) run beside the rest of it, which ends at 2187.4. Much of the 30.3 us of part 3 thus comes from the wait being taken off the end of the routing, and 17 us from the pieces. The prediction's term holds, since before waited for the end; my expectation for this run forgot that.

### Two slot tiles fetched early

```diff
+            pool.wait_ge(q["table_in"], 16)
+            pool.wait_ge(q["w_hi"], 4)
+            pool.wait_ge(q["w_lo"], 4)
+            for t in range(2):
+                fetch_slot(pool, A, T, t, T["XG01"][:, t, :], T["RAW01"][:, t, :], T["x_in01"][t], T["w_in01"][t])
```

> The changed kernel with the tokens and weights of the first two slot tiles fetched while the shared expert still runs (GpSimd issues them behind the table's reading, into the two places where the shared weights lay), and the ring of 6 kept. In the changed kernel 13.0 us pass from GpSimd's first fetch in the slot stage to the first up product, of which 9 us are the weights' transfer. If that transfer is exposed and nothing else comes late: 3.5 to 5 us in place of 13, so 8 to 9.5 us less in the slot stage, the tile staying at 5.1 us. Rival: the third tile, whose fetch still starts with the stage, comes late by as much, so that under 4 us are gained.

2619.8 us (2610.4 to 2622.5, ratio 0.934, 0.932 to 0.935), beside the 2626.4 (2623.1 to 2631.4) of the changed kernel in the same comparison. It is 9.8 us shorter from the graph on by the traces: the last shared product starts at 2297.9, and the timeline goes on

```profile
2299.90 2.00 ACT L2118 ACTIVATE slots_WH<-moe_RAW 128x1024 fp32r<-128x1024 f32 x2 [10.48 <-PEq L48]
...
2304.10 2.04 PE L2196 MATMUL slots_U<-slots_WH,slots_XTH 128*128 128x512 f32 x4 [3.55 <-DVE slots_XTL L2153]
```

From the start of the last shared product to the first up product it is 6.2 us, in place of 15.8 in the changed kernel. The tile stays at 5.10, and the third tile's weights are not waited for, so the rival fell. This version beats both kernels, the changed one by 6.6 us of the medians and 9.8 of the traces. The two intervals (0.932 to 0.935 and 0.935 to 0.939) meet at 0.935, while each of its five runs is faster than each of the changed kernel's five.

## Why the prediction was off

The sum said -155.6 and the spans differ by 192.0; from the graph on, where the change lies, they differ by 178.2. The step that failed is the slot tile in part 6, "I take 5.6", with transfers as what sets it: the tile takes 5.10, set by TensorE, and this is 20 us of the miss. Next comes what the sum had at nothing, the path ahead.

**The path ahead of the changed part (0 predicted, -13.8 measured)** is no effect of the change: it is the cross-attention stage in two single executions, whose end moved with its granted clock. Without it the time would have stood 4 us inside the range (2624.3 + 13.8 = 2638.1); with the slots as summed it would have stood there too. It took both to leave it. The prediction knew that its terms came from one profiled execution, and compared that with the median of three runs. It gave the time no spread for the clock of the untouched 2080 us, while later runs of one kernel on one chip spread over 8 to 24 us. With before at its later median of 2805, the same sum would have given 2649 (2805 - 155.6), inside the range and still 23 us over the later median of the changed kernel.

**Part 6, slots (-62.4 predicted, -82.6 measured).** The gains it named came: the down subtraction is back at 1.23, the ring's waits are gone. What would set the tile then was wrong. "I take 5.6" has transfers as the limit at some 375 GB/s; read from the traces, the transfers' limit is 4.91 us, and TensorE sets 5.10. That is 23 us over 46 steps, of which 3 come off again, since a tile of before took 6.74 and not the 6.81 of the sum. Two bounds were read too high. The stretch of 414 GB/s was the mean of 430 in its first 6 us and 394 in its last 5 (windows 2400 to 2406 and 2406 to 2411), when fewer fetches stood in line. And TensorE's 5.33 was a busy time: in the changed kernel the same 24 operations are busy for 148.0 us in 29.4 tiles, 5.03 each. Why they were busy for longer before was not looked into; stalls counted as busy would explain it. Rival B had the right number at its lower end (5.1, "2634 to 2643"), with a chance of 0.06. The range's floor was B's floor with no room for the clock.

**Part 1 (-4.4 predicted, -7.4).** "Unrolling the four batches itself gains nothing: VectorE shows no gap at a turn" was wrong by 3.0 us: the cost lies for the most part between dependent operations, and 0.13 us a batch at the turn. The split norm is worth 4.4, as summed.

**Parts 2 and 3 (-67.6 predicted, -67.8).** Turning 9.6 (10.4 said), logits 11.3 (10.9 said), then 5.2 to the first shared product (5.3 said). The choice of the high clock held, and rival C fell.

**Parts 4 and 5 (-7.6 predicted, -7.3).** With T the first shared product at 2155.6: counting products at T+24.3 (T+24), counts taken at T+26.6 (T+26.8), the last routing step at T+54.6 (T+55), scatters until T+98 (T+102), last shared product until T+136 (T+136). TensorE stands in one place only, 1.4 us at the counts, and the hole between the halves is gone. Rival E fell.

**Part 7 (-13.6 predicted, -13.1).** Held; the first twelve norm tiles on ScalarE take 0.71 each, not 0.64, and stay hidden.

**The other rivals.** A (the transfers stay the limit) fell; they are the next limit, 0.19 us below. D (POOL locked out) fell: POOL's fetch of tokens does take 1.69 us on average in the slots in place of 0.95 (and 0.94 in fewer_products_and_subtractions, where VectorE's subtractions are short), but POOL waits 1.9 us a tile for a place anyway. The rule of the Trainium skill (SBUF — State Buffer, SBUF: two separate sides), that the shared port pair is an exclusive lock and the one that comes second is held until the first is through, was cited for the fetches alone. Its larger effect is the one undone here and brought back in pool_subtracts, and there the traces agree with it: VectorE's held subtraction ends 1.09 us behind POOL's. For the fetches they show only that they are longer beside such subtractions. F (code fetch) fell: the written-out slots show no gap on TensorE.

## What to carry to other kernels

Before taking a second engine's help for element-wise work on SBUF, look at what the first engine's operations take beside it, each one and not their mean: here the help cost more than it gave, and the deeper ring could not show its worth until the help was gone. When a wait for a transfer goes, the tile falls to the next limit, so read each limit from a stretch where it alone binds: a rate while fetches stand in line throughout, an engine's work from the back-to-back spacing of its operations. And give a forecast for a long kernel the spread of its untouched part: one profile of each kernel may differ by as much as a small change is worth.

## What the runs showed of the hardware

- Products with 16 moving columns did not bring TensorE's clock back from 1.2 GHz in 39 us without a gap in its records (router_moving), where products with 512 moving columns did in about 5 us. Products with 16 standing and 512 moving columns, right behind turns at the high clock, kept it (four in 0.93 us, changed kernel).
- The clock's path through a stage with many short waits is not the same from run to run: the cross-attention stage, the same code, ended between 1037.3 and 1059.1 us in 13 traces, with a mean clock of 0.83 in the two latest and 0.87 to 0.89 in the four earliest.
- A subtraction of 128x1024 SBUF operands on VectorE that meets one on POOL ended 1.09 us behind POOL's: 3.1 to 3.4 us in place of 1.22 (pool_subtracts, 31 of 33), and 2.6 to 2.9 in the kernel before (28 of 29). POOL's takes 2.4 us, 2.7 where it started behind VectorE's.
- Gathers of rows of 12 and 2 KB with stores of 2 KB rows between them reached 427 GB/s on one core's 16 DMA engines (2.10 MB in 4.91 us; 423 by the packets), while a weights' fetch took 18.5 us to land (fewer_products_and_subtractions).
- In a loop over a register, a VectorE operation that waits for the one before it starts 0.09 to 0.12 us later than written out, with no trace in its own duration (before_graph_unrolled; operand or wait, not told apart).
